# The second weighing ahead of q's first projection, and an item of 2816 TensorE instructions

## What is computed

```python
def attn_layer(x, Wqkv, qs, ksc, Wo):
    qkv = x @ Wqkv
    q, k, v = jnp.split(qkv, 3, -1)          # 16 heads of 64 each
    q, k = l2norm(q) * qs, l2norm(k) * ksc
    q = q * cos * scale + rotate_half(q) * sin * scale
    k = k * cos / scale + rotate_half(k) * sin / scale
    sim = einsum(q, keys of the own and the previous window of 32) * 8.0
    attn = softmax(where(mask, -big, sim))
    return (attn @ v).reshape(b, n, INNER) @ Wo

def ffn_layer(x, g, bln, W1, b1, W2, b2):
    xn = layernorm(x) * g + bln
    a, gate = jnp.split(xn @ W1 + b1, 2, -1)
    return a * gelu(gate) @ W2 + b2

for i in range(6):
    x = attn_layer(shift_tokens(x), ...) + x
    x = ffn_layer(shift_tokens(x), ...) + x
```

## Time and profile before

| | |
|---|---|
| median of 3 runs | 1723.12 us (1721.3 to 1727.1) |
| span of the profiled execution | 1725.8 us |
| TensorE busy | 1585.1 us (92%) |
| VectorE busy | 1446.8 us (84%) |
| ScalarE, GpSimd busy | 1117.1 us (65%), 1069.6 us (62%) |
| chain that ended last | TensorE 75%, issue 9%, VectorE 5%, ScalarE 4%, GpSimd 2% |

### The profile page before, as it was taken

How to read it: one execution, slowest core, us unless ns; L and a number is a source line. 1 busy time by engine, 2 the same in 40 slices (tenths; PEclk the granted TensorE clock), 3 DMA queues, 4 the chain that set the end, 5 groups by cost and what they waited for, 6 DMA issues and landing times.

```text
span 1725.8 us, 77157 instructions
## 1 busy us (share of the span) xinstructions
PE 1585.1 (92%) x32762; PEld 1278.6 (74%) x32763; DVE 1446.8 (84%) x3173; ACT 1117.1 (65%) x2014; POOL 1069.6 (62%) x1040
## 2 busy tenths in 40 slices
PE   4569999899999998999999999999999999999987
PEld 2247877777878777778777788777777777877874
DVE  8978988888889887888888889888888888888862
ACT  4346776667667666677666666666766666776663
POOL 3656766666666665667566567476576575665640
PEclk8589999999999999999999999999999999999998
DMA  2111110201111211110211111211111111011110
GB/s 86 31 44 49 40 49 25 77 24 48 44 37 37 65 36 38 41 49 28 67 34 48 41 37 40 61 37 52 38 40 40 49 49 44 29 47 44 33 46 13
DMA packets 41084, 75.06 MB, mean 43 GB/s; under 512 B 9472, under 2 KB 22568, under 8 KB 40744
## 3 DMA queue, kind: packets, MB, share of 16 engines
q1 hardware_dynamic: 40744, 70.12, 14.0%
HBM read 20.08 MB, written 2.10 MB: 13 GB/s over the span
## 4 chain that ended last, share of the span: by engine, by line
PE 75%; issue 9%; DVE 5%; ACT 4%; POOL 2%; ACTq 0%; DVEq 0%; POOLq 0%
PE bank L1359 8%; PE bank L1328 8%; PE bank L1465 8%; PE bank L1396 8%; PE wide L1436 7%; PE bank L1330 7%; PE bank L1329 7%; PE bank L1451 5%; PE bank L1529 4%; PE bank L1414 3%; PE bank L1385 2%; PE bank L1514 2%; PE bank L1515 1%; PE bank L1516 1%; PE bank L1476 1%
## 5 line engine op out<-in xcount | busy, mean ns | idle before, releaser
L864 POOL TENSOR_TENSOR qk<-qk,rnorm 128x512 f32<-128x512 f32 x384 | 401.8, 1046 | 351.0 <-DVE rnorm L1017 351.0
L856 POOL TENSOR_TENSOR qk<-qk,qk_sin 128x512 f32<-128x512 f32 x384 | 492.3, 1282 | 174.6 <-DVE qk_sin L978 174.5
L1180 ACT ACTIVATE squares<-bank 128x512 f32<-128x512 f32 x384 | 229.5, 598 | 152.6 <-DVE qk_sin L978 152.6
L988 DVE TENSOR_REDUCE norm<-squares 128x8 f32<-128x512 f32 x384 | 258.4, 678 | 30.7 <-ACT squares L1180 28.5
L1328 PE MATMUL bank<-w_hi,xs_hi 128*128 128x512 f32 x576 | 264.3, 459 | 12.3 <-ACT squares L1180 7.0
L971 DVE TENSOR_TENSOR qk<-bank,tables 128x512 f32<-128x512 f32 x384 | 261.6, 681 | 9.4 <-PE bank L1330 9.2
L978 DVE TENSOR_TENSOR qk_sin<-bank,tables 128x512 f32<-128x512 f32 x384 | 261.1, 680 | 0.6 <-POOL qk L856 0.6
L1330 PE MATMUL bank<-w_hi,xs_lo 128*128 128x512 f32 x576 | 230.3, 400 | 0.9 <-issue 0.9
L1329 PE MATMUL bank<-w_lo,xs_hi 128*128 128x512 f32 x576 | 229.2, 398 | 1.2 <-issue 1.1
L1359 PE MATMUL bank<-ident,qk 128*128 128x128 f32 x1536 | 226.5, 278 | 3.3 <-POOL qk L864 1.5
L1359 PEld LDWEIGHTS bank<-ident,qk 128*128 128x128 f32 x1536 | 181.0, 142 | 43.5 <-issue 5.0
(11 more groups left out here) (181 smaller groups left out, 2735.8 us busy)
## 6 DMA issues: line engine op xcount, KB each, us to landing
v<-v SPq DMA_DIRECT2D x96, 390.0 KB, 3.5
v<-v SPq DMA_DIRECT2D x72, 130.0 KB, 3.7
w_raw<-in_L_ffn_Wqkv SPq DMA_DIRECT2D x36, 256.0 KB, 3.9
w_o_s<-in_L_ffn_Wo SPq DMA_DIRECT2D x6, 512.0 KB, 5.9
w_raw<-in_L_ffn_W SPq DMA_DIRECT2D x6, 341.0 KB, 4.2
mix_x_nat<-in_L_attn_x SPq DMA_DIRECT2D x4, 256.0 KB, 3.5
w_raw<-x_res_scratch SPq DMA_DIRECT2D x4, 256.0 KB, 3.5
out<-w_raw SPq DMA_DIRECT2D x4, 256.0 KB, 3.1
```

The source lines that it names most:

```text
L856: pool.tensor_tensor(qk[:, g % 2, c, :], qk[:, g % 2, c, :], qk_sin[:, (QK_CHUNKS * g + c) % SINES, :], ALU.add).then_inc(added[c], 1)
L864: pool.tensor_tensor(view, view, rnorm[:, g % 2, c * HPC:(c + 1) * HPC].unsqueeze(2) .to_broadcast([P, HPC, DH]), ALU.mult).then_inc(norme ...
L988: dve.tensor_reduce(norm2[:, c * HPC:(c + 1) * HPC], squares[:, c % 2, :].rearrange("p (h d) -> p h d", d=DH), AX.X, ALU.add).then_inc(sum ...
```

## The change

Two edits, both in TensorE's program. The projection of Q0 moves behind `weigh(step - 3, 1)`, and so also behind `expand(item - 2, 2)` at t = 1 and `centre(item - 1)` at t = 3. And from step 7 on, at t = 0 and t = 3, six of the eight mask products of a score are made as two products of 256 columns each.

```diff
+    FIRST_SPLIT = 7
...
+            def mask_halves(step):
+                return (6, 0, 0, 6)[step % NBLK] if step >= FIRST_SPLIT else 0
...
                 for h in range(4):
                     for r in range(2):
                         row = slice(DH * r, DH * (r + 1))
-                        pe.matmul(bank[4 + r][WINDOW * h:WINDOW * (h + 1), :], ident_bf[row, DH * r:DH * r + WINDOW],
-                                  mask_bf[row, min(g % NBLK, 1), :], start=True, stop=True)
+                        parts = 2 if 2 * h + r < mask_halves(step) else 1
+                        for part in range(parts):
+                            cols = slice(part * CHUNK // parts, (part + 1) * CHUNK // parts)
+                            pe.matmul(bank[4 + r][WINDOW * h:WINDOW * (h + 1), cols], ident_bf[row, DH * r:DH * r + WINDOW],
+                                      mask_bf[row, min(g % NBLK, 1), cols], start=(part == 0), stop=True,
+                                      skip_group_check=(part > 0))
...
                 project(step, V0)
-                project(step, Q0)
                 if t == 1:
                     expand(item - 2, 2)
...
                 weigh(step - 3, 1)
+                project(step, Q0)
```

## The result

The changed kernel takes **1782.6 us** (1779.0 to 1788.9) where the kernel before, beside it, takes 1723.0 (1721.3 to 1727.1): 1.0326 times as long, 95% interval 1.0293 to 1.0359. The forecast was 1765 with a range of 1730 to 1790. The profiled execution spans 1777.3 us, 51.5 more than before's.

What follows compares the result with a forecast made beforehand. TensorE (92% busy) was taken as the bound, VectorE (84%) close behind. New waits and pauses of 4.7 us an item less 2.7 of present pauses, taken as + 1.9 over 22 items, gave 42 us more: 1765 us, range 1730 to 1790.

Steps and rivals of the forecast that it cites:

- A pause is a block that isn't there, and the place makes it: TensorE's score pauses: it runs into an instruction block not yet fetched, where 256 instructions pass quickly; about 2.7 us an item.
- pauses don't follow the blocks: Rival: constant phase changes nothing, pauses stay 2.7 us an item and the new waits come on top; 1787 us, chance 0.05.
- the halves hold the queue: Rival: split masks hold TensorE's queue, + 0.43 us in each of 44 scores, 19 us more, 1784 us; chance 0.08.
- t = 2: 0.3: Scores at t = 2: 3.45 us between block starts against 3.65 wanted, a pause of 0.3 us on average.
- t = 3: 1.7: Turn of o behind the scores at t = 3: window 1.5 us against 3.2, a 1.7 us pause in every item.
- short pause: Rival: at t = 3 the block is asked for early, pause 0.5 us or less; 1734 us, chance 0.16.
- Pauses gone, 2.7 an item, for 2.0 new ones: Whole item: present pauses of 2.7 us vanish; new ones of 0.3 at t = 2 and 1.7 at t = 3 come.
- t = 0: + 0.5: VectorE's rotate(0) at t = 0 waits for the later Q0, making TensorE later too; 0.5 us on average.
- t = 1: + 1.3: Masks at t = 1: rotate(0) 1.73 us later delays gate(2), which frees their banks; TensorE waits 1.3 us more.
- t = 2: VectorE 0.5 late: Maxima at t = 2: VectorE ready 0.5 us after the scores let go, reaching TensorE at V1 through squares(2).
- t = 3: + 0.6: At t = 3 Q0 stands behind centring and weighing, so the scores come 0.6 us later on TensorE.
- The sum: Per item: 4.7 us of new waits and pauses less 2.7 of present pauses, + 2.0, taken as + 1.9.

Runs made afterwards that it cites:

- order_only: The changed kernel with all masks whole, Q0 still behind the weighing, so the block starts drift again; 1783.7 us, 1.0360 of the kernel before.
- halves_only: The kernel before with only the halved masks added, Q0 staying ahead of the weighing; 1729.5 us, 1.0049 of the kernel before.
- after_phase100: The changed kernel with 81 more mask products once in steps 4 to 6, moving later block starts 94 instructions further on; 1760.9 us.
- mixed_100: mixed_6 with 81 more mask products once, moving later block starts 94 instructions further on; 1706.7 us, 0.9904 of the kernel before.
- mixed_6: The changed kernel with weighing ahead of Q0 only at t = 1 (Q0 ahead of the expansion) and t = 2; 1745.1 us.
- q0_t1: The changed kernel with weighing and Q0 ahead of the expansion at t = 1, other steps as they were; 1748.4 us.
- mixed_112: mixed_6 with 75 more mask products once, moving later block starts 106 instructions further on; 1736.3 us, 1.0082 of the kernel before.

## Why the prediction was right, and where not

The direction, the range and the cause of the new waits (Q0 comes late for VectorE) hold; that the order and not the halves costs is shown by order_only and halves_only. The number was 18 us low, and that it lies no further off is in part luck: the pauses at t = 2 and t = 3 were each far off, in opposite directions. By its own steps:

- **A pause is a block that isn't there, and the place makes it.** Right: after_phase100 gained 22 us on the changed kernel and mixed_100 38 on mixed_6, each by another place of the same order. The rival "pauses don't follow the blocks" came near in time (1787) but falls with these. Nearer still was "the halves hold the queue" (1784), which falls with order_only: without the halves the time is the same. The Trainium skill ("Runtime: NRT & Kernel Launch", section "Instruction fetch mechanics") says that crossing a block is mostly hidden; mixed_6 and mixed_100 do the same work but for 81 small products and are 38 us apart, so here it is not.
- **No pause at t = 0 and 1.** Right, 0.00 in both.
- **t = 2: 0.3.** This is the step that failed: measured 1.87. I counted the time from the start of the block, 3.65 us, taken from windows of the kernel before. It holds from the start of the packet, 2.45, and that starts at 1.1 us in the kernel before's order but at 2.0 when the weighing stands ahead of Q0. Typical are 1.25 in the scores and 0.27 at the block start in the weighing; the rest are the five items that load weights, which I hadn't counted.
- **t = 3: 1.7.** Measured 0.89, mostly 0.50. Also the packet: the sequencer asks ahead of the block's start here. This is the mechanism of the rival "short pause", which came true at t = 3 and was undone at t = 2.
- **Pauses gone, 2.7 an item, for 2.0 new ones.** 2.80 for 2.76.
- **Halves: 0.03 a split score.** Right in size: masks at 743.48, scores at 743.71, 0.23 us for 0.22; halves_only has 0.01 to 0.03 a step in the median. Its single long steps, 0.4 us an item, were not foreseen.
- **t = 0: + 0.5.** 0.53.
- **t = 1: + 1.3.** 1.18; the masks wait 1.00 us, 22 times, for the gate. q0_t1 takes it away and 34 us with it.
- **t = 2: VectorE 0.5 late.** Not seen, 0.23 in the mean and nothing in the median: the scores' pause covers it. In after_phase100, where that pause is mostly gone, it shows: at t = 2 TensorE's K1 waits for ScalarE's squares, its first weight load starts 0.64 us after the load before it for 0.23 (medians), and the median of the rest is 13.68 for 13.32. The place is K1, where I had named V1.

```profile
722.81 0.19 PEld L1329 LDWEIGHTS bank<-w_hi,xs_hi 128*128 128x128 f32 x1 [0.46 <-ACT squares L1181]
```

- **t = 3: + 0.6.** 0.34.
- **The sum.** New waits 2.28 where I had 2.7, pauses unchanged where I had them 0.7 less; + 2.24 for + 1.9. The errors of the two pauses partly cancelled. The last step, the median from the profiled span, was off as well: the changed kernel's profiled execution is 5.3 us under its median, before's was 2.7 over its own. That is 8 of the 18 us.

What I said would show it: pauses of L1405 under 10 us was wrong (38.7), the gate wait and the 93 waits for Q0 came as named, and one pause an item in o's turn at t = 3 came, at half the length.

## What to carry to other kernels

Read from which point an engine's stop is timed: here it is the packet of instructions, 2.45 us, and not the start of its block; a stretch of short instructions stalls by what the packet is late, and the order of the work around it can make it late (1.1 or 2.0 us at t = 2, from 0.35 ahead to 1.1 behind at t = 3). In a reordering look first at who reads the result that is pushed back; if that engine works through a fixed order, the wait comes back where its next results are due (here at the masks of the same step). And where a loop body is a whole number of instruction blocks, its time depends on where the body starts in a block, 38 us here, so two orders are to be compared at several places each.

## What I had not expected of the hardware

- A fetch of 16 KB mostly takes 0.9 to 1.45 us on its queue (the longest 2.0), and where TensorE stops for it, it goes on 2.2 to 3.0 us (once 3.3) after the packet's start.
- Where TensorE stops for it, the packet starts anywhere from 0.5 us ahead of the preceding block's start to 5.3 behind it (in order_only, at the weighing of t = 2, up to 6.9). The centring right ahead of Q1 goes with a packet 1.4 us later, queues full of weights with one 2 us later; nine late ones in mixed_112 and five in after_phase100 come with idle queues and stay open.
- A pause of over 2.2 us often costs 1.55 more in the same step: in halves_only in six of seven, in the changed kernel in all five at t = 2 and in none of three at t = 3. Why is open.
- The same program but for 81 products of a few columns at its start: 1783 or 1761 us.
